# Attention scores by Strassen's seven products in a cross-attention block on one Trainium2 core

## What is computed

```python
memory_proj = jnp.einsum('bme,de->bmd', memory, W_mem)
scores = jnp.einsum('bnd,bmd->bnm', hidden_states, memory_proj) / jnp.sqrt(jnp.float32(D))
attn = jax.nn.softmax(scores, axis=-1)
memory_context = jnp.einsum('bnm,bmd->bnd', attn, memory_proj)
gate_input = jnp.concatenate([hidden_states, memory_context], axis=-1)
gate = jax.nn.sigmoid(jnp.einsum('bnf,df->bnd', gate_input, W_gate) + b_gate)
fused = hidden_states + gate * memory_context
return _rmsnorm(fused, norm_w)
```

## Time and profile before

| | us |
|---|---|
| median of 3 runs (1547.89 to 1550.29) | 1548.31 |
| the profiled execution | 1548.15 |
| its span | 1546.4 |
| PE busy in the span | 1526.7 |
| DVE / ACT / POOL busy | 1083.8 / 549.9 / 33.3 |

### The profile page before, as it was taken

One profiled execution on the slowest core, in us unless ns is written; L12 is line 12 of the kernel. 1 busy time (PEld: TensorE's weight loads), 2 busy tenths in 40 slices (PEclk: granted clock), 3 DMA queues, 4 the chain that ended last, 5 costly groups with the idle time before them and its releaser, 6 DMA issues.

```text
span 1546.4 us, 21062 instructions
## 1 busy us (share of the span) xinstructions
PE 1526.7 (99%) x6720; PEld 1262.5 (82%) x6720; DVE 1083.8 (70%) x1518; ACT 549.9 (36%) x929; POOL 33.3 (2%) x72
## 2 busy tenths in 40 slices
PE   7999999999999999999999999999999999999997
PEld 6888888888888878888888888888888888888886
DVE  6565758777777874577436674577555898899987
ACT  4333342222222352244222432244222554444443
POOL 0000000000000000000000000000000011111111
PEclk9999999999999999999999999999999999999999
DMA  9999426333332786667566756667758645455553
GB/s 185 221 237 226 118 89 187 110 109 109 109 109 101 164 218 167 165 154 194 157 171 170 188 138 182 167 153 196 184 150 272 226 173 197 196 196 197 195 198 120
DMA packets 221979, 262.68 MB, mean 170 GB/s; under 512 B 34032, under 2 KB 144624, under 8 KB 221680
## 3 DMA queue, kind: packets, MB, share of 16 engines
q1 hardware_dynamic: 221936, 262.21, 60.6%
HBM read 170.39 MB, written 89.65 MB: 168 GB/s over the span
## 4 chain that ended last, share of the span: by engine, by line
PE 97%; DMA 1%; DVE 1%; SPq 1%; ACT 0%; issue 0%; POOL 0%; DVEq 0%; POOLq 0%; ACTq 0%
PE bank L1656 58%; PE bank L1703 20%; PE bank L1811 19%; DMA region_f<-in_ctx 1%; SPq L257 0%; DMA prob<-in_L_xattn_W_gate 0%; SPq L345 0%; ACT prob L840 0%; DVE region_n L311 0%; DVE region_f L1377 0%; ACT region_n L824 0%; POOL mean_sq L709 0%; SPq L352 0%; DVE region_f L1369 0%; SPq L459 0%
## 5 line engine op out<-in xcount | busy, mean ns | idle before, releaser
L1656 PE MATMUL bank<-region_n,region_l 128*128 128x512 f32 x1536 | 353.6, 389 | 1.0 <-DVE region_n L311 1.0
L1656 PE MATMUL bank<-region_t,region_l 128*128 128x512 f32 x1536 | 353.0, 389 | 0.0
L1656 PEld LDWEIGHTS bank<-region_n,region_l 128*128 128x128 f32 x1536 | 288.2, 188 | 61.4 <-issue 1.4
L1656 PEld LDWEIGHTS bank<-region_t,region_l 128*128 128x128 f32 x1536 | 288.4, 188 | 59.8
L1656 PE MATMUL bank<-region_t,region_n 128*128 128x512 f32 x960 | 220.1, 392 | 8.2 <-DVE region_n L311 7.4
L1656 PEld LDWEIGHTS bank<-region_t,region_n 128*128 128x128 f32 x960 | 181.5, 189 | 46.4 <-DVE region_t L311 8.6
L858 ACT CAST region_l<-bank 128x512 fp32r<-128x512 f32 x128 | 75.0, 587 | 339.8 <-DVE bank L1310 339.5
L311 DVE TENSOR_TENSOR region_t<-region_f,region_t 128x1024 fp32r<-128x1024 f32 (+2 forms) x83 | 111.1, 1372 | 65.8 <-ACT region_t L730 57.3
L1703 PE MATMUL bank<-region_t,region_l 128*128 128x512 f32 x576 | 135.7, 389 | 0.0
L1703 PEld LDWEIGHTS bank<-region_t,region_l 128*128 128x128 f32 x576 | 108.1, 188 | 22.4
L1310 DVE STREAM_TRANSPOSE bank<-region_f 128x512 f32<-128x512 f32 x128 | 88.7, 715 | 50.3 <-DMA region_f<-prob_scratch 48.0
(11 more groups left out here) (90 smaller groups left out, 1478.8 us busy)
## 6 DMA issues: line engine op xcount, KB each, us to landing
region_f<-in_ctx SPq DMA_DIRECT2D x128, 256.0 KB, 5.2
prob_scratch<-prob SPq DMA_DIRECT2D x128, 256.0 KB, 2.7
region_f<-prob_scratch SPq DMA_DIRECT2D x128, 256.0 KB, 4.5
region_f<-in_x SPq DMA_DIRECT2D x64, 256.0 KB, 5.7
region_f<-in_x SPq DMA_DIRECT2D x128, 128.0 KB, 2.8
region_f<-in_x SPq DMA_DIRECT2D x16, 1024.0 KB, 4.9
out<-region_f SPq DMA_DIRECT2D x31, 512.0 KB, 2.7
q_scratch<-prob SPq DMA_DIRECT2D x8, 1024.0 KB, 7.9
```

Source lines behind the costliest of these rows:

```text
L1656: mm = nc.tensor.matmul(dst, lhs(a), rhs(b), start=first and n == 0, stop=last and n == len(PASSES) - 1)
```

## The change

The scores are no longer formed block by block for one unit, but for a **pair of units against half of the memory** (1024 rows), by Strassen's seven products. Call that a **round**: 4 pairs, 2 halves and 4 batches make 32 rounds. A product has 2 tiles of the contraction in 3 passes, 6 matmuls; a round has 42 matmuls where two units against two blocks had 48.

- **Left operands.** A set has 11 blocks of 128x256 kept as HI and LO in three groups (two raw blocks, four sums, one raw block). POOL forms the four sums (`q_sums`) and the LO of the three groups (`q_lo`), ACT the HI (`q_hi`). A batch needs six sets: four for the first half, and two more where a pair returns in the second half.
- **Right operands.** For each half, the seven blocks `w_transpose`, `w_sums`, `w_hi_of` and `w_lo` (four transposes of 128x1024, four sums, seven splits). Half of the sums are POOL's. The weights of stage C go the same way.
- **Softmax by halves.** Each half has its own maximum (in the second half the larger of both), its own exponentials, now 128x1024, and its own sum. The products with the two halves of the memory go to two banks, and `first_half` (ACT) and `join_halves` (DVE) add them with weights that `weights_of_halves` works out once for a pair.
- **Order.** All eight rounds of a batch come first, then all eight `with_memory`, the first half's score round before the second's. Loops over units are written out. The last unit's `with_memory` now stands before all gate products. Product 7 of a round is put off into the round behind it.

```diff
+            def strassen(ps, x, w, opens, closes, signal):
+                for t in range(CH):
+                    for m, (a, b) in enumerate(PASSES):
+                        mm = nc.tensor.matmul(ps, x[:, a, P * t:P * (t + 1)], w[:, b, t, :],
...
+            def scores(b, h, k):
+                score_product(b, h, k, 1)
+                score_product(b, h, k, 2)
+                if k:
+                    score_product(b, h, k - 1, 7)
+                elif h:
+                    score_product(b, 0, PPB - 1, 7)
+                for n in (3, 4, 6, 5):
+                    score_product(b, h, k, n)
...
+            for b in range(NB):
+                for h in range(2):
+                    for k in range(PPB):
+                        scores(b, h, k)
+                for i in range(UPB):
+                    for g in range(MB):
+                        with_memory(b, i, g)
+                        if i == 0 and g == 0:
+                            score_product(b, 1, PPB - 1, 7)
```

On ACT, in each round (`fill` holds the splits of operands that are wanted later):

```diff
+            def scores_act(b, h, k, fill):
+                seed_b(b, h, k)
+                keep_22(b, h, k)
+                fill(0)
+                keep_12(b, h, k)
+                if k:
+                    exps(b, h, k - 1, 1)
+                elif h:
+                    exps(b, 0, PPB - 1, 1)
+                fill(1)
+                exps(b, h, k, 0)
```

`seed_b` copies a 128x512 bank to another one, `keep_22` and `keep_12` copy a bank to SBUF. On DVE:

```diff
+            def scores_dve(b, h, k, fill):
+                before = (b, h, k - 1) if k else (b, 0, PPB - 1) if h else None
+                if before is not None:
+                    add_last(*before)
+                fill(0)
+                if before is not None:
+                    close_1(*before)
+                fill(1)
+                close_0(b, h, k)
+                fill(2)
```

On POOL:

```diff
+            def q_sums(L):
...
+                nc.gpsimd.tensor_tensor(s1, a21, a22, ALU.add).then_inc(uq_sum, 1)
+                nc.gpsimd.tensor_tensor(s3, a11, a21, ALU.subtract).then_inc(uq_sum, 1)
+                pool.wait_ge(uq_sum, 4 * L + 1)
+                nc.gpsimd.tensor_tensor(s2, s1, a11, ALU.subtract).then_inc(uq_sum, 1)
+                pool.wait_ge(uq_sum, 4 * L + 3)
+                nc.gpsimd.tensor_tensor(s4, a12, s2, ALU.subtract).then_inc(uq_sum, 1)
+
+            def q_lo(L, *ids):
+                for n in ids:
+                    pool.wait_ge(uq_hi, 3 * L + n)
+                    v = left_group(L, n)
+                    nc.gpsimd.tensor_tensor(v[:, LO], q_group(L, n), v[:, HI].bitcast(F32), ALU.subtract
+                                            ).then_inc(uq_ready, 1)
```

More of the change, by code:

```diff
@@ new lines, in gemm_of, with left_of, left_set, left_pair @@
+        def gemm_of(b, h, pair):
+            return [gemm(b, h, k) for k in range(PPB) if pair_of(b, h, k) == pair][0]
+        def left_of(b, h, k):
+            if h == 0:
+                return LPB * b + k
+            return LPB * b + (pair_of(b, h, k) if k < 2 else k + 2)
+        def left_set(L):
+            b, l = divmod(L, LPB)
+            return (l + 1) % 2 if b == 0 or l >= PPB else l % 2
+        def left_pair(L):
+            b, l = divmod(L, LPB)
+            return l if l < PPB else pair_of(b, 1, l - 2)
@@ L1764, in step_pe @@
-            def step_pe(i, next_mt=None, own_mn=None, softmax=True):
-                if softmax:
-                    pe.wait_ge(uq_ready, i + 2)
-                    for j in range(MB):
-                        pe.wait_ge(exp_done, i * MB + j + 1)
-                        if next_mt is not None:
-                            pe.wait_ge(mt_ready, next_mt * MTS + HPJ * (j + 1))
-                        scores(i + 1, j)
-                pe.wait_ge(am_ready, i)
-                with_memory(i, own_mn)
```

1404 lines of the change are left out of this document (805 added, 599 removed).

## The result

The changed kernel takes **1565.41 us** (median of 3, 1563.07 to 1566.37) against 1548.31: the medians are 17 us apart, slower, where I forecast 21 us less. The ratio on record is 1.0102, with a 95% interval of 1.0087 to 1.0116. The profiled execution took 1563.07 us. By the prediction's own sum the new waits are S = 1563.07 - 1503.6 = **59.5 us**, not 23.7.

What follows compares the result with a forecast made beforehand. PE was taken as the bound, busy 1526.7 of 1546.4 us. From 1548.15, 43.5 for 192 matmuls and 1.0 for a stop gave 1503.6; new waits of 23.7 made 1527.3, taken as 1527, range 1506 to 1546.

Steps and rivals of the forecast that it cites:

- S: All new waits of PE, (a) to (e) added together: 23.7 us on top of the floor.
- (a): Gate stage to scores: product 2 of the first round waits for DVE's last evacuation, 4.0 us.
- (b): First change of halves, first batch: extra splits on DVE and ACT's late memory split hold product 5, 2.0 us.
- (c): Second halves: POOL holds DVE's memory split, so `add_last` comes 1.3 us late eight times, 10.4 us.
- rival 2: Late transfers: DMA queues full in second halves, 2 to 5 us in each batch, 1535 to 1547 us; chance 0.15.
- (d): Scores to products, four batches: first units' transposes wait on DVE and the weights' chain, 1.2 us each, 4.8 us.
- (e): End of attention: product 5 waits for two evacuations behind four splits of the context weights, 2.5 us.
- The floor: Whole kernel without new waits: 1548.15 less 43.5 for 192 matmuls and 1.0 for a stop, 1503.6 us.
- Rival 1: In attention, DVE isn't held by POOL: (c) goes and (a) is 2.0, 1515 us; chance 0.28.
- rival 3: First half of a batch: POOL becomes the bound, 9 us a batch at 3 times DVE's time, 1578 us; chance 0.12.
- The joints cost nothing: Between batches: no new wait, because the next right operands are ready two units ahead.

## Why the prediction was wrong

By its own steps, with PE's gaps of after sorted by place:

| Term | Forecast | Gaps in after, us |
|---|---|---|
| (a) gate stage to scores | 4.0 | 0.87 + 1.68 = 2.6 |
| first half of batch 0, behind the entry | 0 | 0.69 + 0.69 + 2.07 + 0.38 = 3.8 |
| (b) first change of halves | 2.0 | 0 |
| (c) second halves | 10.4 | 2.4 + 2.7 + 3.3 + 3.0 = 11.4 |
| late stores, batches 1 to 3 | rival 2 | 5.8 |
| third round of a first half, batches 1 to 3 | 0 | 2.6 |
| (d) scores to products | 4.8 | 3 x 3.37 + 1.1 = 11.2 |
| (e) end of attention | 2.5 | 1.4 |
| half clock | 0 | 17.1 / 2 = 8.5 |

A stop costs more than its idle time, at both ends. A group of six matmuls takes 1.52 us in a stream and 1.63 to 1.67 behind a gap; over 39 gaps that adds about 5.5 us. And the last matmul before a gap is listed with 0.389 us where the next would have started after 0.227; the gap is counted from its end only, so 39 x 0.162 = 6.3 us more are lost. 38.7 + 8.5 + 5.5 + 6.3 = 59.0 of the 59.5 us. The sum of the prediction had room for idle time alone.

**The floor was right.** 6528 matmuls; with POOL's part taken away the kernel ran at 1513.9, 10 us above 1503.6. The saving is there.

**DVE held by POOL: right, and not carried through.** (c) rested on it and came out at 11.4 for 10.4, but that the sums agree is luck. I gave 1.3 us at two places of each second half. At the third round's product 7 there are 1.0 to 1.1; at the fourth round's, nothing. The rest stands where I had put nothing: 0.4 at the second round's product 7, 0.6 to 1.0 at the last one in three batches, and 0.7 at product 2 of the fourth round, for a LO of POOL. (a) is near in size as well, but its 1.68 us are a wait for POOL's LO and not for DVE's evacuation. Rival 1 fell. POOL at twice DVE was right as well: 128x1024 takes 2.37 to 2.40 us undisturbed, 256 columns 0.73. So rival 3, which ended on the right side, did not happen by its mechanism of a POOL at 2.6 times DVE or more. That POOL's length costs PE's time at all is right even so, and I gave it nothing at twice: with DVE's hold on it, it is worth up to 31 us where DVE itself is almost free.

**The step that failed most is (d)**, in the sentence that a unit takes 10.9 us, DVE needs 8.7, "and no more waits follow". I priced the weights' chain at 1.5 us from undisturbed steps. The same paragraph put POOL's four sums of 128x1024 nowhere, though POOL's list has them right behind the batch's last left set, and they start when DVE's transposes are done (649.42), just where the chain of the second pair of units runs. I asked of the hold what it does to operations of 1024 and 2048 columns, where it doubles them. A step of 0.16 us becomes 2.3. The earlier trace rows showed exactly that on the other engine: an add on one column that took 0.65 for 0.19. That is 6.4 us more in gaps than (d) allowed and (3.4 + 3.4 + 6.8) / 2 = 6.8 of half clock behind them, 13.2 together; the run with only the weights changed gives 14.4. That is over a third of the 35.8 us by which S was too small. The others are terms that the sum put at nothing: the two ends of each stop (11.8), the late stores (5.8), the entry's first half (3.8), the third rounds (2.6) and the rest of the half clock (1.7); (c) was 1.0 larger, and (a), (b) and (e) came out 4.5 us smaller.

**The clock was left out.** I took 1.00 for the whole kernel since before had it. Before had one gap of 1.02 us in attention. A change that makes gaps has to ask.

**"The joints cost nothing"** was right of the joints. The third round of a first half, where POOL owes most, did cost: rival 3's place, at 2.6 us where it had 36.

**Late transfers (rival 2)** came true in part: 5.8 us of gaps in three batches. The DMA engines are full in the burst around the late store (shares of 0.92 and 1.05), as this rival said, though not in the stage as a whole. Moving the store ahead in the same burst removes these gaps, and so does taking POOL's work away; so a full burst alone does not make them.

**Range.** 1546 left out this case. The hold and late transfers stood in the text as alternatives with chances of their own, but nothing kept them apart, and they came together. The half clock stood nowhere in it.

## What to carry to other kernels

Before an engine gets background work that reads two tensors, list every small two-tensor operation of DVE on the critical chain, and give it one tensor and a per-partition scalar: here 0.2 to 0.3 us instead of up to 2.3, and 25 us of 1565. A stop of PE costs its length, some 0.3 us more at its two ends, and behind the longer ones (2.07 and 3.35 to 3.38 us in after) a stretch at half clock too; useless matmuls in it can be cheaper. Read the DMA share of the stretch in which a transfer is late, not that of the stage. Fix gaps by reading who stood ahead of the late instruction on its own engine, one edit at a time: two edits that were put in unseen beside two good ones cost 14 us (1545.5 against 1531.4).

## What the runs showed of the hardware that I had not expected

- A DVE `tensor_tensor` on one or two columns waits to the end of the GpSimd two-tensor operation beside it (2.30 us for 0.16). With one tensor and scalars from SBUF it takes 0.20 to 0.27 on average beside the same work.
- A GpSimd operation with one tensor input mostly leaves DVE alone (2.285 us for 128x2048, as undisturbed; the exceptions reach 1.03 us for a step of 0.15), but is slower than the two-tensor one: 2.78 against 2.37 us for 128x1024.
- The granted clock stood at 0.50 for 3.4 or 6.8 us at gaps of PE. In attention, in all traces from after on, it did so at all of the 13 longest gaps (2.97 to 4.28 us), at 16 of the next 21 (1.96 to 2.81 us), and at none of the others (1.82 us and less).
- A store of 512 KB that was issued behind eight loads of 256 KB took 9.3 us to land, at a DMA share of 1.05; the median is 5.1.
